# Attention stage with a list of steps for each engine, k scaled on ScalarE, and the loads, the side work and the last unit rearranged

## The reference

```
x = x + conv_stack(norm(x))      # 4 small layers, 64 channels
x = x + ffn(norm(x))             # silu(gate) * up, 1792 wide; each weight is w * (su @ sv)
x = x + attention(norm(x))       # 32 query heads, 8 key/value heads, head size 128
x = x + ffn(norm(x))             # the same weights again

# attention, per sequence and key/value head (a group of 4 query heads)
q, k, v = x @ Wq.T, x @ Wk.T, x @ Wv.T
q = q * rsqrt(mean(q*q) + eps) * q_norm_w
k = k * rsqrt(mean(k*k) + eps) * k_norm_w
attn = softmax(q @ k.T / sqrt(128) + slope[head] * (pos_k - pos_q), causal)
x = x + (attn @ v) @ Wo.T
```

## Time and profile before

| | |
|---|---|
| three runs | 2678.17 us median (2675.16 to 2679.56) |
| the profiled execution | 2672.38 us, its span 2671.1 us |
| PE busy | 2436.2 us (91% of the span) |
| DVE, ACT, POOL busy | 1735.9, 1141.6, 790.2 us |
| granted clock of PE, mean | 0.979 |
| DMA | 444.97 MB, mean 167 GB/s |

### The profile page before, as it was taken

One profiled execution on the slowest core, in us unless ns is written; L12 is line 12 of the kernel. 1 busy time (PEld: TensorE's weight loads), 2 busy tenths in 40 slices (PEclk: granted clock), 3 DMA queues, 4 the chain that ended last, 5 costly groups with the idle time before them and its releaser, 6 DMA issues. The chain is left out here.

```text
span 2671.1 us, 40780 instructions
## 1 busy us (share of the span) xinstructions
PE 2436.2 (91%) x12810; PEld 2034.4 (76%) x12810; DVE 1735.9 (65%) x4087; ACT 1141.6 (43%) x3658; POOL 790.2 (30%) x1204
## 2 busy tenths in 40 slices
PE   6899999899698898998988989999999987999999
PEld 4677777678587777877777777888888776887887
DVE  7656666542277677777777777777777776556554
ACT  6433333321155455555555555555555543113121
POOL 4621444320033334333333343333333332002000
PEclk9899999999899999999999999999999998999999
DMA  4245569986520533434345235224233213545554
GB/s 150 72 158 201 204 233 368 408 322 244 215 83 29 209 119 150 185 119 164 145 154 217 107 143 205 82 84 181 73 135 123 98 42 111 208 179 201 188 203 152
DMA packets 86578, 444.97 MB, mean 167 GB/s; under 512 B 9368, under 2 KB 16664, under 8 KB 66656
## 3 DMA queue, kind: packets, MB, share of 16 engines
q1 hardware_dynamic: 85008, 440.91, 43.9%
q10 hardware_dynamic: 1360, 1.46, 0.2%
HBM read 342.72 MB, written 99.61 MB: 166 GB/s over the span
## 5 line engine op out<-in xcount | busy, mean ns | idle before, releaser
L763 PE MATMUL psum<-qw,xs 128*128 128x384 f32 x2688 | 520.8, 344 | 17.8 <-DMA qw<-weff_q 15.7
L763 PEld LDWEIGHTS psum<-qw,xs 128*128 128x128 f32 x2688 | 464.3, 190 | 20.3 <-issue 18.1
L2318 POOL TENSOR_SCALAR prob<-prob,rsum 128x128 f32<-128x128 f32 (+1 forms) x512 | 212.1, 427 | 429.3 <-DVE rsum L2418 415.0
L2233 ACT ACTIVATE squares<-cc 128x128 f32<-128x128 f32 x512 | 154.6, 305 | 369.0 <-DVE cc L2375 246.1
L763 PE MATMUL psum<-wo_h,oT_h 128*128 128x512 f32 x512 | 219.8, 429 | 94.6 <-DVE oT_l L2426 75.9
L2265 ACT ACTIVATE prob<-biased,nmax 128x256 f32<-128x256 f32 (+1 forms) x512 | 227.5, 446 | 167.2 <-DVE nmax L2408 167.1
L763 PE MATMUL psum<-wo_l,oT_h 128*128 128x512 f32 x512 | 203.9, 398 | 0.0
L763 PE MATMUL psum<-wo_h,oT_l 128*128 128x512 f32 x512 | 203.6, 398 | 0.0
L763 PEld LDWEIGHTS psum<-wo_h,oT_h 128*128 128x128 f32 x512 | 98.1, 192 | 134.1 <-DVE oT_l L2426 91.5
L2426 DVE TENSOR_TENSOR oT_l<-psum,oT_h 128x512 fp32r<-128x512 f32 x128 | 88.3, 690 | 144.1 <-ACT oT_h L2277 144.1
L2385 DVE SCALAR_TENSOR_TENSOR cc<-cc,rr,kw 128x128 f32<-128x128 f32 x128 | 95.8, 787 | 112.5 <-POOL rr L2308 112.5
(11 more groups left out here) (318 smaller groups left out, 6090.2 us busy)
## 6 DMA issues: line engine op xcount, KB each, us to landing
xs<-weff_x SPq DMA_DIRECT2D x62, 1792.0 KB, 7.8
wgu<-weff_gu SPq DMA_DIRECT2D x42, 1024.0 KB, 7.9
weff_q<-q_parts SPq DMA_DIRECT2D x56, 768.0 KB, 4.0
qw<-weff_q SPq DMA_DIRECT2D x56, 768.0 KB, 8.1
wD<-weff_dn SPq DMA_DIRECT2D x56, 512.0 KB, 4.9
wS<-weff_s SPq DMA_DIRECT2D x28, 1024.0 KB, 6.8
wdn<-weff_dn SPq DMA_DIRECT2D x42, 512.0 KB, 4.3
weff_gu<-wgu SPq DMA_DIRECT2D x14, 1024.0 KB, 4.2
```

Of the source, the lines that this page charges most:

```text
L763: ins = pe.matmul(out_ap, stat[a], mov[b], start=start and n == 0, stop=stop and n == last)
L2233: ins = act.activation(squares[:, first_place + hd, :], cc[:, tile, half, (hd + 1) * HD:(hd + 2) * HD], ACT.Square, accum_out=ss[:, n:n + 1])
L2318: pool.tensor_scalar(prob[:, b, lo:hi], prob[:, b, lo:hi], rsum[:, b, t:t + 1], 1.0, ALU.mult, ALU.mult).then_inc(prob_done, 1)
```

## The change

1. **A list for each engine.** `order2` becomes five lists. `UNIT_STEPS` gives each engine's steps in a unit; `besides` adds what only some units have.
2. **k.** `ksc` moves from DVE to ACT and multiplies by the inverse root alone. The norm weight, now one number for each partition, is applied after the transposition: as the scale of ACT's copy `kThi`, and in DVE's `kTlo`, which becomes a scalar_tensor_tensor. The semaphore of `ksc` and `qsc` 0 becomes two.
3. **Sums paced by chunk.** In phase 1, `turn_of` ties each set and each row of a sequence to the gate step of a chunk: 1.25 of them for each chunk, from chunk 28 on, a group's sets before two sequences. `GROUPS1` falls from 4 to 3 and so `MADE_AHEAD` from 3 to 2: five groups' sets (3 to 7) are made in phase 2.
4. **First loads ahead of the barrier.** SP waits for the saved sums alone, then loads sequence 0, the sets that lie below phase 1's `wgu0` (five of seven by the layout), sequence 1, the output weights and the norm weights, and only then passes `phase1_over` and loads the other two sets.
5. **The last unit.** Its steps and the preparation of phase 3 are ordered by a second use of the planner, attention first (urgency 1 against 2 and 3).
6. Products run as 1, 7, 6, 5, 2, 4, 3.

```diff
-        GROUPS1, QRING = 4, 3
+        GROUPS1, QRING = 3, 3
...
+            written = 0.0
+            def turn_of(size):
+                nonlocal written
+                chunk = 2 * IC + int(written / 1.25)
+                written += size
+                return [("gsilu", chunk, 0)]
...
-                    o.add(("qhi", g, e), "act", 0.85, [("qcomb", g, e - 3) if e > 2 else (("qf", g, 0), 7.0)] + (
+                    o.add(("qhi", g, e), "act", 0.85, [("qcomb", g, e - 3) if e > 2 else (("qf", g, 0), 7.0)] + turn_of(1.0) + (
...
-                    o.add(("arow", q, j), "dve", 0.55, left + [("inv", 2, q)], 6, ("row", 1))
+                        o.add(("arow", q, j), "dve", 0.55, left + [("inv", 2, q)] + (turn_of(0.9)), 6, ("row", 1))
...
-        PRODUCTS2 = (1, 6, 7, 5, 2, 4, 3)
+        PRODUCTS2 = (1, 7, 6, 5, 2, 4, 3)
...
+        UNIT_STEPS = {
+            "pe": "sc0 sc1 sc2 sc3 pr1 pr7 pr6 pT0 pT1 pr5 pr2 pr4 set0 at0 pr3 pT2 pT3 set1 outa0 at1 outa1 kT0 qT1 qT0 "
+                  "out0 out1",
+            "dve": "bias0 bias1 rsum0 bias2 rsum1 bias3 u2 pTlo0 u3 pTlo1 c22 c11 rsum2 rsum3 u4 c21 set0 oTlo0 c12 rows pTlo2 "
+                   "pTlo3 qsc0 oTlo1 set1 vlo0 qTlo1 qTlo0 kTlo0 oadd0 oadd1",
+            "act": "set0 exp0 exp1 exp2 prcopy0 pThi0 pThi1 exp3 sq5 sq2 rows oThi0 sq4 pThi2 pThi3 sq3 ksc0 oThi1 vhi0 set1 qThi1 "
+                   "kThi0 qThi0",
+            "pool": "set0 norm0 norm1 sums norm2 norm3 nrm1 nrm0 qsc1 set1",
+            "sp": "sets0 set0 sets1",
+        }
...
+        EARLY_SETS = [j for j in range(7) if placed[f"qw{j}"] + 8 * SET <= placed["wgu0"]]
+        order2 = {e: [] for e in UNIT_STEPS}
+        order2["sp"] += [("lqw", 0, j) for j in range(7) if j not in EARLY_SETS]
+        order2["pool"] += [("rel", 0, 0)]
+        for u in range(-1, UNITS - 1):
+            for e in UNIT_STEPS:
+                order2[e] += unit_steps(e, u)
...
+        closing = Steps({})
+        u = UNITS - 1
+        for hd in range(GRP):
+            closing.add(("sc", u, hd), "pe", 0.59, [], 1)
+            closing.add(("bias", u, hd), "dve", 0.93, [("sc", u, hd)], 1)
...
+            closing.add(("frow", 0, j), "dve", 0.55, last[:1], 2)
+            closing.add(("fxT", 0, j), "pe", 0.5, [("frow", 0, j)] + last[1:], 2)
...
+                closing.add(("plo", 0, q), "dve", 1.1, [("phi", 0, q), ("flo", 0, q + TPB)], 3)
+        order_closing = closing.ordered()
...
         def sp_phase2():
+            stack_left(sp)
+            sums_saved(sp)
+            load_rows(0)
+            for j in EARLY_SETS:
+                load_set(0, j)
+            load_rows(1)
+            load_output_weights(0)
+            sp.dma_start(qkw, qk_w).then_inc(small_in, 16)
             phase1_over(sp)
-            sp.dma_start(qkw, qk_w.partition_broadcast(P)).then_inc(small_in, 16)
...
+                elif what == "ksc":
+                    act.wait_ge(r_done, 2 * a + 1)
+                    for t in range(STILES):
+                        ins = act.activation(cc[:, t, 0, 0:HD], cc[:, t, 0, 0:HD], ACT.Copy, scale=rr[:, t:t + 1])
+                    ins.then_inc(k_sc, 1)
...
-                    act.activation(kT[0], psum[:, KV, 0:SEQ], ACT.Copy).then_inc(kT_hi, 1)
+                    act.activation(kT[0], psum[:, KV, 0:SEQ], ACT.Copy, scale=kw[:]).then_inc(kT_hi, 1)
...
-                    for t in range(STILES):
-                        ins = dve.scalar_tensor_tensor(out=cc[:, t, 0, 0:HD], in0=cc[:, t, 0, 0:HD], scalar=rr[:, t:t + 1],
-                                                       in1=kw, op0=ALU.mult, op1=ALU.mult)
...
-                    dve.tensor_tensor(kT[1], psum[:, KV, 0:SEQ], kT[0].bitcast(F32), ALU.subtract).then_inc(kT_lo, 1)
+                    dve.scalar_tensor_tensor(out=kT[1], in0=psum[:, KV, 0:SEQ], scalar=kw[:], in1=kT[0].bitcast(F32),
+                                             op0=ALU.mult, op1=ALU.subtract).then_inc(kT_lo, 1)
```

More of the change, by code:

```diff
@@ L1778, in pe_phase1, with sums_saved @@
                     pe_ffn(what, a, b)
+        def sums_saved(engine):
+            engine.wait_ge(s_out, 32 * IC)
+            for n in range(SETS1 - WSLOTS, SETS1):
+                set_saved(engine, n)
+            engine.wait_ge(xs_out, 32 * SEQS1)
         def phase1_over(engine):
@@ L1785, in phase1_over @@
             engine.wait_ge(inv_done[2], 2 * (NBLK - 1))
[L1786 to L1789, removed]
+            sums_saved(engine)
         def sb3(name, shape, dt=F32, where="phase3"):
@@ L1964, in hybrid_block @@
-        A_DVE = counts(k for k in order1["dve"] + order2 if k[0] in ("arow", "alo"))
-        A_ACT = counts(k for k in order1["act"] + order2 if k[0] in ("aev", "ahi"))
-        A_TILE = counts(k for k in order1["pe"] + order2 if k[0] == "axT")
-        SUMS2 = ("u2", "u3", "c22", "u4", "c11", "c21", "c12")
+        UNIT_STEPS = {
[8 rows of a table added]
+        }
+        SUMS2 = ("u2", "u3", "c22", "c11", "u4", "c21", "c12")
+        PROJECTING = ("pr", "prcopy", "sum", "sq", "nrm", "ksc", "qsc", "vhi", "vlo", "kT", "kThi", "kTlo", "qT", "qThi", "qTlo")
@@ new lines, in unit_steps @@
+        def unit_steps(engine, u):
+            for name in UNIT_STEPS[engine].split():
+                if name in SUMS2:
+                    step_ = ("sum", u + 1, name)
+                elif name in ("set0", "set1", "sums", "rows", "sets0", "sets1"):
+                    if u >= 0:
+                        yield from besides(engine, name, u)
+                    continue
+                else:
+                    step_ = (name[:-1], u + (name[:-1] in PROJECTING), int(name[-1]))
+                assert step_[0] in PROJECTING or step_[0] in ATTENDING
+                if 0 <= step_[1] < UNITS:
+                    yield step_
@@ new lines, in hybrid_block @@
+        for k in range(2):
+            closing.add(("at", u, k), "pe", 1.03, [("pTlo", u, 2 * k + 1)], 1)
+            closing.add(("oThi", u, k), "act", 0.5, [("at", u, k)], 1)
+            closing.add(("oTlo", u, k), "dve", 0.61, [("oThi", u, k)], 1)
+            closing.add(("outa", u, k), "pe", 1.39, [("oTlo", u, 0)] + ([("outa", u, 0)] if k else []), 1)
+        for k in range(STILES):
+            closing.add(("out", u, k), "pe", 1.39, [("outa", u, k), ("oTlo", u, 1)] + ([("out", u, 0)] if k else []), 1)
+            closing.add(("oadd", u, k), "dve", 0.61, [("out", u, k)], 1)
@@ L1983, in region2 @@
             return psum[:, REGION2[m], 0:KVQ // 2]
-        wo_bank = [e for e in order2 if e[0] == "axT" or (e[0] == "outa" and e[2] == 1) or (e[0] == "pr" and e[2] == 6)]
+        wo_bank = [e for e in order2["pe"] if e[0] == "axT" or (e[0] == "outa" and e[2] == 1) or (e[0] == "pr" and e[2] == 6)]
         def wait_spare(e):
@@ new lines, in load_output_weights @@
+        def load_output_weights(g):
+            for half in range(2):
+                if g:
+                    sp.wait_ge(wo_lo, 2 * (g - 1) + half + 1)
+                if g == 1:
+                    sp.wait_ge(a_dve, A_DVE["alo", BATCH - 1, 0])
+                elif g > 1 and g - 1 + MADE_AHEAD < KVH:
+                    sp.wait_ge(w_comb, 4 * (IC + g + MADE_AHEAD))
+                sp.dma_start(stage[:, half, 0:GRP // 2 * DM],
+                             wo[g][:, half * GRP // 2 * DM:(half + 1) * GRP // 2 * DM]).then_inc(wo_in[half], 16)
```

311 lines of the change are left out of this document (144 added, 167 removed).

## The result

The changed kernel takes 2487.79 us (median of four runs, 2483.88 to 2492.3) where the kernel before took 2676.66 in the same comparison: a ratio of 0.9295, with a 95% interval of 0.9275 to 0.9314. Forecast were 2500 us and a range of 2470 to 2575.

The account below looks back on a forecast made before the run. PE, busy 91% of the span, was taken as the bound, so mainly its waits could be won. Attention -134, phase 1 -15, barrier -18 and last unit -11 made -178: span 2493, forecast 2500 us, range 2470 to 2575.

Parts of the forecast that it names:

- Plain unit: Attention's units without side steps: 20.4 us from scores to scores instead of 22.1 (ends 20.0 and 21.2).
- The walk: Step-by-step timing of a plain unit from old times, counted from its first score matmul; next scores at 20.4 us.
- The forecast wait of 0.3 us: In the plain unit, PE waits 0.3 us before `out` 0, which starts at 17.5, for oT's low part.
- Other units: Attention beyond 63 plain units: 38 us, from units 4 and 5, sets, and the rest at 10 us.
- Units 4 and 5: Two attention units with the same sequence chain as before, high copy now ahead of `qT`'s copies: +19 us.
- Sets: Attention units that make sets, five groups instead of four: 0.6 us in two units, 0.3 in two, 9 us altogether.
- Phase 1: Phase 1 with sums paced by chunk: 15 of 20 us taken as won (bounds 0 and -24).
- The gap: Barrier to first scores: early loads let the seventh product end 11 us after the barrier; -18 us (bounds -10, -24).
- The closing stretch: Last unit's first scores to phase 3's first product: 30 us with DVE 80% filled, -11 (bounds -5 and -15).
- Rival 1: The plain unit's wait only moves, the last 4 us being serial: units of 21.2, 2550 us; chance 0.15.
- Rival 2: Phase 1 and the barrier give nothing: 33 us come back, 2533 us; chance 0.07.
- rival 3: Slower: in attention a late `norm` 0 on POOL holds up the projections, units of 23.3, some 2690 us; chance 0.03.

Follow-up runs that it names:

- e1: Changed kernel with phase 1's sums made as before, unpaced, and four groups in attention instead of five: 2498.9 us, ratio 0.9336.
- e7: Changed kernel with the two late sets issued right behind the barrier, ahead of sequence 1, the output weights and qk_w: 2480.28 us, ratio 0.927.
- e4: Changed kernel with k's scaling, weight included, back on DVE, each engine's own list kept: 2496.48 us, ratio 0.9306.
- e14: Changed kernel with attention's steps in the old common order, side steps at old places, k scaled on DVE: 2641.18 us, ratio 0.9857.
- e9: Changed kernel with one common order for all engines and k scaled on DVE, side steps at new places: 2680.93 us, ratio 1.0002.
- e11: Changed kernel with qk_w, then the late sets, loaded earlier, and sequences 6 and 7's high and low parts made at units' ends: 2465.05 us, ratio 0.9198.

## Why the prediction was right

The sum of the stages was forecast at -178 us and came out at -185.7, the difference of the two spans. The mechanisms in attention held, but part of the agreement is luck: attention and phase 1 gave 10.2 and 8.0 us more than forecast, the gap and the closing stretch 6.8 and 2.2 less.

- *Plain unit*: forecast 20.4 us, measured 20.2. The walk's steps stand in the rows above, from the unit's start at 1907.00: the first root ends at 13.7 (forecast 13.7), the second at 15.1 (15.0), `qsc` 1 at 16.1 (16.1), `qsc` 0 at 16.7 (16.8). That DVE's `qsc` 0 and POOL's `qsc` 1 run beside each other and DVE's stands still was right (1.53 us against 0.68 in the earlier trace rows); I had taken 1.7. The forecast wait of 0.3 us before `out` 0 is there, but it is 0.16 us and stands in the weight loads only, because oT's low part is ready at 17.3, not 17.5. 63 times 0.2 us is 12.6 us, more than the whole difference in attention (forecast -134, measured -144.2), so the side steps cost 2 us more than forecast. `ksc` on ACT was sized too small (0.395 us, not 0.30), and hidden all the same. `kTlo` was 0.474 where 0.48 was taken.
- *Other units*: 1313.0 less 63 times 20.2 is 40.4 us; forecast 38. Units 4 and 5: 59.9 less 40.4, so +19.5 against +19. Sets: 8.4 us in five groups against 9, a sum that agrees better than its terms: 0.8 us in two groups and 2.0 to 2.5 in three, where 1.8 was forecast for each.
- *Phase 1*: forecast -15, measured -23.0, near the bound of -24. I held back 5 of the 20 us without a row for it; PE was never idle in the window where it had stood for 14.8 us, and e1 shows that the way in which the sums are made is the whole of it.
- *The gap*: forecast -18, measured -11.2. This term was the worst. The first product came at once, as forecast, but I let the last two sets land "at 8 to 10" us and the seventh product end at 11; they landed at 14.1 and 15.9 behind the barrier, and it ended at 18.4. What failed is the start of the loads: I let the last save be over 16 us ahead of the barrier, and it was over 11.3 us ahead, having taken 7.7 us to land. The loads themselves took 27.3 us from the first issue to the last landing, against the 26 that I reckoned (16 and 10), so 4.7 of the 6 us are the late start. The forecast had counted sequence 1 and the output weights ahead of the two sets, so that order, which e7 shows to cost 4.3 us of the gap, is a gain I passed over and not the error. e1 bears this out: with the loads 19.2 us ahead, behind one another in the same order, the two sets landed 6.6 and 8.4 us behind the barrier.
- *The closing stretch*: forecast -11, measured -8.8; DVE was busy for 25.5 us in it, not 23.6, and 78% filled, not 80%.
- *Phase 3*: +1.5 us, taken as nothing.
- The profiled execution lies nearer to the median of the runs than before: 2485.4 of span against 2487.79, 2.4 us where 7.1 were added. That is 4.7 of the 12.2 us between forecast and result; the other 7.5 or so are the stages.

Rival 1 (the wait only moves, units of 21.2) was wrong: 0.16 us are left of the 1.2. But oT's low part still releases `out` 0, so whatever delays that chain by a little lengthens the unit (20.4 us in e4). Rival 2 fell with phase 1's 23 us, rival 3 because POOL's `norm` was not late: PE waits for it 13 times in the whole changed kernel, 5.9 us together. What the prediction did not say, and the runs did, is how much of attention's gain of 158.8 us (from e14) either of two edits has alone: the lists 151.5, k's move 101.0.

## What to carry to other kernels

When several edits of one change act on one wait, undoing them one at a time understates all of them: here undoing k's move alone costs 7.3 us of attention, doing it alone brings 101.0. Undo both as well, and check that the twin of the old kernel takes the old time before reading differences off it; e9 did not, because the side steps had been left at new places. And where loads are moved ahead of a barrier, put those on which the next products wait in front of the bulk, small ones like qk_w first of all. Where PE's rows show no idle time, look at the weight loads too before calling a wait gone.

## What the hardware showed that was not expected

A 128x128 copy on ACT took 0.395 us with its scale read per partition, where squares of the same size took 0.30; the 128x256 copy from PSUM for kT took 0.469 with such a scale and 0.368 before, without it. DVE's `qsc` 0 took 1523 to 1531 ns all 64 times beside POOL's of 1045, where it took 0.68 alone. The two start 0.06 to 0.07 us apart every time, and the price of that neighbour is the same 0.85 us in every unit, not a spread. And a load of 1 KB that is issued behind large ones took 19.0 us to land in the changed kernel, 13.9 in e7, and 7.4 in e11, where only sequence 0 was ahead of it:

```profile
stage<-in_qk_w SPq DMA_DIRECT2D x1, 1.0 KB, 7.4
```
